# Loading each edge tile's query rows from DRAM in a two-layer graph transformer on one Trainium2 core

## What is computed

```
# layer 0                                    # layer 1 (edges carry 64 features)
h = layer_norm(x); q, k, v = h@Wq, h@Wk, h@Wv    q, k, v = x@Wq, x@Wk, x@Wv; e = edge_attr@We
logit = sum(q[dst] * k[src], -1) / 4             logit = sum(q[dst] * (k[src] + e), -1) / 4
p = exp(logit - segment_max(logit, dst)[dst])    the same
alpha = p / segment_sum(p, dst)[dst]             the same
agg = segment_sum(alpha * v[src], dst)           agg = segment_sum(alpha * (v[src] + e), dst)
x = x + agg@Wo + bo                              x = x + norm(x + agg + x@Wskip + ...) etc.
x = x + gelu(layer_norm(x)@W1 + bf1)@W2 + bf2    feed-forward with norms
```

## Time and profile before

| | |
|---|---|
| time, median of 3 runs | 1712.79 us (1712.45 to 1723.33) |
| profiled execution | 1715.09 us, of which 1713.4 us are the span from the first instruction to the last |
| TensorE busy, matrix products | 1117.7 us, 65% |
| VectorE / ScalarE / GpSimd busy | 1070.8 us, 62% / 842.6 us, 49% / 897.7 us, 52% |
| DMA | 222.70 MB, mean 130 GB/s |
| edge loop of the first layer | from about 60 to 762 us |
| edge loop of the second layer | from about 862 to 1610 us |

### The profile page before, as it was taken

One profiled execution on the slowest core, in us unless ns is written; L12 is line 12 of the kernel. 1 busy time (PEld: TensorE's weight loads), 2 busy tenths in 40 slices (PEclk: granted clock), 3 DMA queues, 4 the chain that ended last, 5 costly groups with the idle time before them and its releaser, 6 DMA issues. The chain is left out here.

```text
span 1713.4 us, 27206 instructions
## 1 busy us (share of the span) xinstructions
PE 1117.7 (65%) x6771; PEld 999.6 (58%) x6771; DVE 1070.8 (62%) x2749; ACT 842.6 (49%) x2617; POOL 897.7 (52%) x1001
## 2 busy tenths in 40 slices
PE   3504666656656666778941678777686777778675
PEld 2304566656656655667821667666575676767674
DVE  5505666666765666785710766667666676766866
ACT  1203554555565555574510255455545555555775
POOL 3572665666566666403467065655555555554044
PEclk9756876787778877788975878788878878777888
DMA  5642454445545544420133255545555554544101
GB/s 162 135 131 86 126 160 151 127 156 164 151 132 159 159 128 154 146 100 10 54 117 105 90 163 151 168 146 175 153 160 160 153 163 155 158 144 147 64 2 38
DMA packets 100397, 222.70 MB, mean 130 GB/s; under 512 B 34859, under 2 KB 49482, under 8 KB 96669
## 3 DMA queue, kind: packets, MB, share of 16 engines
...
## 5 line engine op out<-in xcount | busy, mean ns | idle before, releaser
L487 POOL DMA_INDIRECT KV<-kv_table,idx x832 | 803.6, 966 | 573.0 <-issue 459.3
L784 PE MATMUL PS<-QT,OHT 128*128 x1664 | 420.7, 342 | 291.0 <-issue 143.1
L784 PEld LDWEIGHTS PS<-QT,OHT 128*128 128x128 f32 x1664 | 331.8, 246 | 323.1 <-issue 321.6
L785 PE MATMUL PS<-QT,OHT 128*128 x1664 | 407.3, 334 | 16.2 <-issue 15.9
L785 PEld LDWEIGHTS PS<-QT,OHT 128*128 128x128 f32 x1664 | 334.0, 248 | 18.6 <-issue 18.6
L616 ACT ACTIVATE AGG<-AGG,PC,RCS x800 | 309.3, 387 | 2.5 <-ACT AGG L612 1.7
L1096 DVE TENSOR_TENSOR KV<-KV,PS 128x1024 f32<-128x1024 f32 x104 | 125.9, 1210 | 252.3 <-remote 204.2
L608 ACT ACTIVATE PC<-PS 128x4 f32<-128x4 f32 x200 | 34.2, 171 | 495.7 <-PE PS L830 243.5
L830 PE MATMUL PS<-OH,KV 128*128 128x128 f32 x1600 | 235.9, 296 | 45.1 <-issue 29.9
L830 PEld LDWEIGHTS PS<-OH,KV 128*128 128x128 f32 x1600 | 217.3, 211 | 52.8 <-issue 49.7
L1103 DVE TENSOR_TENSOR PR<-KV,PS 128x512 f32<-128x512 f32 x208 | 141.0, 678 | 157.0 <-issue 86.8
...
## 6 DMA issues: line engine op xcount, KB each, us to landing
...
```

The lines of the kernel that those rows point to most:

```text
L487: g.indirect_dma_start(KV[:, s, j, :], None, kv_table, bass.IndirectOffsetOnAxis(ap=idx[:, s, j:j + 1], axis=0)).then_inc(gathered[s][hh], 16)
L784: te.matmul(o, OHT[:, q // 2, 0, e0:e0 + P], QT[:, ds(blk, P)], start=True, stop=False)
L785: last = te.matmul(o, OHT[:, q // 2, 1, e0:e0 + P], QT[:, ds(blk + P, P)], start=False, stop=True)
```

## The change

The queries of a block no longer stay on the chip. `projected` and `next_queries` write them to one of four slots (`q_out`), and `store` sends them to a second DRAM table, `q_table`, of 3328 rows of 512 bytes. `rel` is now the distance from the destination of the tile's own first edge, 0 to 127. `load_queries(n)` on SyncE reads the first nodes of the 16 tiles into registers (two loads of eight) and issues 16 DMAs, each of the 128 rows of `q_table` from that node on, into one half of the double-buffered `QW`. With that the tile needs one one-hot matrix of 128 rows and one product. `OHT` has half the size, `one_hots1` one instruction where it had two, `one_hots` two where it had four. TensorE loads no registers, and waits for `q_loaded` before every eight tiles.

```diff
@@ -46,7 +46,7 @@
...
     rel_dram = nc.dram_tensor("rel_dram", (G, J * P), BF16, kind="Internal").ap()
-    block_dram = nc.dram_tensor("block_dram", (G, J), I32, kind="Internal").ap()
+    q_table = nc.dram_tensor("q_table", (NP + P, D), F32, kind="Internal").ap()
     window_dram = nc.dram_tensor("window_dram", (G, P, J * P), F32, kind="Internal").ap()
@@ -60,10 +60,10 @@
...
         Y = sb("Y", [P, NP])
-        QT = sb("QT", [P, NP + P])
+        QW = sb("QW", [P, 2, J, D])
         AGG = sb("AGG", [P, NP + P])
         KV = sb("KV", [P, SLOTS, J, 2 * D])
-        OHT = sb("OHT", [P, 2, 2, 8 * P])
+        OHT = sb("OHT", [P, 2, 8 * P])
         OH = sb("OH", [P, J * P])
@@ -143,7 +142,7 @@
...
         hT2 = [tail[:, 8 + k, D:2 * D] for k in range(2)]
-        hL = [tail[:, 10 + k, 0:D] for k in range(2)]
+        q_out = [tail[:, 10 + k, 0:D] for k in range(4)]
         last_windows = KV[:, (G - SLOTS) % SLOTS, 0:J // 2, :].rearrange("p j d -> p (j d)")
@@ -153,13 +152,12 @@
...
-        dst_edge = OHT[:, 1, 1, 0:T].bitcast(I32)
+        dst_edge = QW[:, 1, 0:4, :].rearrange("p j d -> p (j d)")[:, 0:T].bitcast(I32)
         prep = kv_flat[:, 2 * J * 2 * D:3 * J * 2 * D]
...
         relC = prep[0:TP, 1538:1794].bitcast(BF16)
-        blkC = prep[0:TP, 1794:1798].bitcast(I32)
         firstC, samerC, loopC, sameC = [prep[0:TP, 1798 + n * P:1798 + (n + 1) * P].bitcast(U8) for n in range(4)]
@@ -305,13 +304,13 @@
...
-            sp.wait_ge(*done("rel_made", 2))
+            sp.wait_ge(*done("consts_made", 16))
+            sp.dma_start(q_table[NP:NP + P, :], PM[:, :]).then_inc(S["pad_stored"], 16)
+            sp.wait_ge(*done("rel_made", 1))
             sp.dma_start(flat(rel_dram).rearrange("(p n) -> p n", p=TP), relC).then_inc(S["rel_stored"], 16)
-            sp.dma_start(flat(block_dram).rearrange("(p n) -> p n", p=TP), blkC).then_inc(S["rel_stored"], 16)
             sp.wait_ge(*done("gate_made", 3))
             sp.dma_start(gate_dram, gate_rows).then_inc(S["gate_stored"], 16)
-            sp.wait_ge(S["rel_stored"], 32)
-            sp.dma_start(block_row[:, :], row(flat(block_dram))).then_inc(S["block_loaded"], 16)
+            sp.wait_ge(S["rel_stored"], 16)
             sp.wait_ge(S["gate_stored"], 16)
@@ -320,9 +319,12 @@
...
                     sp.dma_start(kv_table[ds(n * P, P), :], kv_out[k]).then_inc(kv_stored[k], 16)
+                    sp.wait_ge(*done("q_made", n + (l * NB + 1)))
+                    sp.sem_inc(S["sp_go"], 1)
+                    sp.dma_start(q_table[ds(n * P, P), :], q_out[k]).then_inc(kv_stored[k], 16)
                 def stored(n, k):
-                    sp.wait_ge(kv_stored[k], n * 4 + (16 - 4 * k + 16 * kv_uses[k] * l))
+                    sp.wait_ge(kv_stored[k], n * 8 + (32 - 8 * k + 32 * kv_uses[k] * l))
                     sp.sem_inc(S["kv_free"], 1)
...
                 def indices(n):
@@ -333,10 +335,19 @@
...
                 def places(n):
-                    sp.wait_ge(*done("oht_ready", n * 2 + 2 * G * l))
-                    sp.wait_ge(*done("oht2_ready", n * 2 + 2 * G * l))
+                    sp.wait_ge(*done("oht_ready", n + G * l))
+                    sp.wait_ge(*done("oht2_ready", n + G * l))
                     sp.sem_inc(S["sp_go"], 1)
                     sp.dma_start(REL[:, :], rel_dram[ds(n, 1), :].broadcast_to([P, J * P])).then_inc(S["rel_loaded"], 16)
+
+                def load_queries(n):
+
+                    for hh in range(2):
+                        first = values(first_row, n * J + 8 * hh, 8, ENG.SP, N)
+                        sp.wait_ge(*done("qe_ready", 4 * n + (4 * G * l - 6 + 2 * hh)))
+                        sp.sem_inc(S["sp_go"], 1)
+                        for m in range(8):
+                            sp.dma_start(QW[:, n % 2, 8 * hh + m, :], q_table[ds(first[m], P), :]).then_inc(q_loaded[n % 2][hh], 16)
                 def row_gates(n):
@@ -379,7 +390,13 @@
...
                 pipelined(sp, (store, 2), (stored, 0), slots=4)
+                if l == 0:
+                    sp.wait_ge(S["pad_stored"], 16)
+                    sp.wait_ge(S["block_loaded"], 16)
+                    sp.wait_ge(*done("rel_made", 2))
+                load_queries(0)
                 places(1)
+                load_queries(1)
                 if l == 0:
@@ -408,6 +425,8 @@
...
                         store_windows(n - 1)
+                    if n + 2 < G:
+                        load_queries(n + 2)
@@ -436,7 +455,7 @@
...
             g.memset(SUG[:, :], 0.0).then_inc(S["consts_made"], 1)
-            g.memset(QT[:, NP:NP + P], 0.0).then_inc(S["consts_made"], 1)
+            g.memset(PM[:, :], 0.0).then_inc(S["consts_made"], 1)
             g.memset(minus_big[:, :], -BIG).then_inc(S["consts_made"], 1)
@@ -473,7 +492,7 @@
...
                 for k in range(4):
-                    pool.wait_ge(kv_stored[k], 16 * kv_uses[k] * (l + 1))
+                    pool.wait_ge(kv_stored[k], 32 * kv_uses[k] * (l + 1))
                 def gather(n):
@@ -588,11 +607,9 @@
...
                     act.wait_ge(*done("qe_ready", n * 4 + 4 * G * l))
-                    for nf in range(2):
-                        sc.activation(OHT[:, 1, nf, :], REL[:, 8 * P:16 * P], ACT.Abs, bias=minus_part[:, nf:nf + 1]).then_inc(S["oht2_step"], 1)
-                    for nf in range(2):
-                        act.wait_ge(*done("oht2_step", n * 2 + (2 * G * l + nf + 1)))
-                        sc.activation(OHT[:, 1, nf, :], OHT[:, 1, nf, :], ACT.Relu, bias=one_col[:, 0:1], scale=-1.0).then_inc(S["oht2_ready"], 1)
+                    sc.activation(OHT[:, 1, :], REL[:, 8 * P:16 * P], ACT.Abs, bias=minus_part[:, 0:1]).then_inc(S["oht2_step"], 1)
+                    act.wait_ge(*done("oht2_step", n + (G * l + 1)))
+                    sc.activation(OHT[:, 1, :], OHT[:, 1, :], ACT.Relu, bias=one_col[:, 0:1], scale=-1.0).then_inc(S["oht2_ready"], 1)
@@ -670,9 +687,9 @@
...
-                act.wait_ge(S["rel_stored"], 32)
-                act.wait_ge(*done("rel_made", 3))
-                act.wait_ge(S["block_loaded"], 32)
+                act.wait_ge(S["rel_stored"], 16)
+                act.wait_ge(*done("rel_made", 2))
+                act.wait_ge(S["block_loaded"], 16)
                 warm(ACT.Exp)
@@ -764,25 +781,20 @@
...
                         skip_part(b, w)
-                pe.wait_ge(S["block_loaded"], 32)
                 pe.wait_ge(*done("q_made", NB * (l + 1)))
...
-                blks = [None] * 8
-
                 def queries_of(n, q):
...
                     if q % 2 == 0:
-                        blks[:] = values(block_row, n * J + 4 * q, 8, ENG.PE, NP - P)
-                        pe.wait_ge(*done("oht2_ready" if q // 2 else "oht_ready", n * 2 + (2 * G * l + 2)))
+                        pe.wait_ge(*done("oht2_ready" if q // 2 else "oht_ready", n + (G * l + 1)))
+                        pe.wait_ge(q_loaded[n % 2][q // 2], 128 * (n // 2 + 1 + G // 2 * l))
                     pe.wait_ge(*done("prod_done", n * 4 + (4 * G * l + q - 1)))
                     for m in range(4):
-                        blk = blks[q % 2 * 4 + m]
                         o = PS[q % 2][:, m * P:(m + 1) * P]
                         e0 = ((4 * q + m) % 8) * P
-                        te.matmul(o, OHT[:, q // 2, 0, e0:e0 + P], QT[:, ds(blk, P)], start=True, stop=False)
-                        last = te.matmul(o, OHT[:, q // 2, 1, e0:e0 + P], QT[:, ds(blk + P, P)], start=False, stop=True)
+                        last = te.matmul(o, OHT[:, q // 2, e0:e0 + P], QW[:, n % 2, 4 * q + m, :], start=True, stop=True)
                     last.then_inc(S["qe_ready"], 1)
...
                 def edge_part(n, q):
@@ -992,13 +1004,11 @@
...
             before_edge, edge_dst, after_edge = [tiles(dstC[:, n:n + TK * P]) for n in range(3)]
-            v.tensor_scalar(blkC, edge_dst[:, :, 0], 7, 7, ALU.logical_shift_right, ALU.logical_shift_left).then_inc(S["rel_made"], 1)
             v.tensor_tensor(tiles(sameC), edge_dst, before_edge, ALU.is_equal).then_inc(S["loops_step"], 1)
...
             v.tensor_tensor(passC, edge_dst[:, :, P - 1], before_edge[:, :, 0], ALU.is_equal).then_inc(S["loops_step"], 1)
-            dve.wait_ge(*done("rel_made", 1))
-            v.tensor_tensor(tiles(relC), edge_dst, blkC.unsqueeze(2).broadcast_to([TP, TK, P]), ALU.subtract).then_inc(S["rel_made"], 1)
+            v.tensor_tensor(tiles(relC), edge_dst, edge_dst[:, :, 0:1].broadcast_to([TP, TK, P]), ALU.subtract).then_inc(S["rel_made"], 1)
             dve.wait_ge(*done("loops_step", 4))
@@ -1072,8 +1082,8 @@
                 def projected(n, k):
...
                     dve.wait_ge(*done("proj_ready", n + 1))
-                    v.scalar_tensor_tensor(QT[:, ds(n * P, P)], o[:, 0:D], 0.25, BB[:, 0:D], ALU.mult, ALU.add).then_inc(S["q_made"], 1)
                     dve.wait_ge(*done("kv_free", n - 3))
```

(8 more changed lines are left out.)

6 lines of the change are left out of this document (3 added, 3 removed).

## The result

The changed kernel took 1692.1 us (median of 4 runs, 1685.2 to 1698.0) where the kernel before took 1713.4 (median of 4): the ratio is 0.9855, with an interval of 0.9823 to 0.9887. That is 21 us less, where 53 were forecast. Its profiled execution took 1693.75 us, 1692.0 of them span.

What follows compares the result with a forecast made beforehand. The prediction took TensorE, held while GpSimd issues gathers, to set a half batch's pitch of 12.3 us. Its terms, -5 - 33 - 13 - 5 - 7 + 9 + 1 = -53 us, gave 1660 us, range 1612 to 1710.

Steps and rivals of the forecast that it cites:

- a hold: Both edge loops: while GpSimd issues gathers, TensorE's results come late, until 1.3 to 1.6 us after the last gather's issue.
- Store of the queries, +9: First stage: SyncE's extra store for each of 25 blocks makes VectorE wait 0.35 us a block, +9 us.
- First layer, steady, -5: First layer's 43 steady halves: GpSimd waits as before, only the excess over a 12.35 us pitch goes, -5 us.
- my third rival: With fewer records the hold misses the sums, GpSimd's first-layer waits shrink too; 1610 us, chance 0.07.
- Second layer, steady, -33: Second layer's 43 steady halves: shorter long waits remove three quarters of 45 us, -33 us (bounds 0 and -45).
- So 0: SyncE's 16 row loads a batch: issued early enough for the rows to land in time, so no cost.
- my fourth rival: SyncE's row loads hold TensorE as gathers do, some 4 us in 43 batches: +170 us, about 1830, chance 0.07.
- Start of the second layer's loop, -13: Fewer query records ahead of VectorE's first products, so the fourth comes at 946, not 956: -13 us (0 to -25).
- Start of the first layer's loop, -5: VectorE's fourth product moves from 137 towards 117, but the gather burst doesn't move: -5 us (0 to -12).
- Last rounds, -7, and the last store, +1: Both loops' rounds without gathers save -7 us (0 to -12); between the layers only the last query store shows, +1 us.
- The clock: TensorE's granted clock falls with half the queries gone, shrinking the second layer's 33 us gain to 5; about 1690, chance 0.12.
- The second rival: Gathers don't hold TensorE; the pitch is GpSimd's and something else ends the wait; 1710 us, within 1%, chance 0.14.

Runs made afterwards that it cites:

- c1: The changed kernel itself, run again beside the kernel before: 1703.9 us against 1731.1, ratio 0.9845.
- e9: The changed kernel with the second layer's first two edge parts of a batch moved behind the first half's sums on TensorE: 1696.7 us, ratio 0.9886.
- e2: The kernel before with one more 64 KB store behind each block's store, to a table nothing reads: 1377.0 us, ratio 1.0091.
- e7: The kernel before with the second query product of each tile left out (numbers differ): 1672.4 us against 1716.2, ratio 0.9751.
- e10: The changed kernel without the row loads of batches 2 to 25, products using old rows (numbers differ): 1683.4 us, ratio 0.9812.
- e8: The changed kernel with a 128 x 1 memset on GpSimd behind each gather, which left the gathers' spacing at 1.25 us: 1692.2 us, ratio 0.9868.
- e5: The changed kernel with GpSimd waiting for VectorE's query-key products before each eight gathers in each layer's first four batches: 1703.6 us, ratio 0.9829.
- e4: The changed kernel with SyncE's edge-gate stores and loads put ahead of places(1) and load_queries(1): 1372.1 us, ratio 1.0061.

## Why the prediction was wrong in size

- **What bounds the kernel: right where there is a hold.** In the changed kernel, in c1 and in e9 the first layer's pitch stays at 12.3 to 12.5 us although TensorE lost 74 us of work (in the changed kernel's profile). But I took the hold for a property of the kernel and of gathers. Gathers alone don't make it: three chips ran the same gathers at the same 1.25 us and held neither TensorE nor SyncE, and the kernel before takes 1364 us there.
- **Store of the queries, +9: right.** +10.0 in the result, first gather 10.5 us later in e2.
- **First layer, steady, -5: right in the result (-8.0), and partly by luck.** Products alone give 7.4 (e7). With the row loads left out it is +10 (e10), where sums that are early make GpSimd run two bursts together. I had argued that GpSimd "waits as before"; with less work on TensorE it sometimes doesn't. That can cost time: where the sums come early in e10 the layer gets slower, and not faster as in my third rival. In e7 early sums mostly cost nothing. When they cost is open.
- **Second layer, steady, -33: the step that failed is "So 0" for the row loads.** The relief itself was sized too low if anything: with everything that the change removes and no row loads the 43 halves take 39.6 us less (576.2 to 536.6, e10), close to my bound of 45; the products alone give 24.2 (e7), so by subtraction the halved one-hots and the register loads on TensorE are worth the other 15, where I had counted one one-hot of 0.75 us. The loads took 22.0 of the 39.6 back (558.6 against 536.6; 23.1 against e8 on the same chip). I had asked whether the rows land in time, and they do: in this loop the profile puts no wait of a product down to them. I hadn't asked what 16 more issues do to the others. With them the segment sums are made after TensorE is let go in 14 of 22 batches, without them in none of the 21 ahead of the last (7.3 us against 3.7 to alpha). This comes nearest to my fourth rival, to which I gave 0.07, at a quarter of its price and in one layer alone: 0.5 us a half, 1 us a batch, and not 4. I had also said there that the loads have as many packets as the gathers. They have three times as many, 144 a load against 48 a gather (110592 packets of SyncE's queue are missing from e10 with its 768 loads; the 832 gathers have 39936). That the loads cost the 22 us is shown by e10; how they do it is argued from these timelines, and whether their number or their packets count isn't shown. In the whole time little of it is seen: without the loads the kernel would gain 6 to 9 us, not 22, since the first layer gets slower. So the loads aren't the whole miss: the next item (11 us) and the last rounds (6 us) make half of it.
- **Start of the second layer's loop, -13: mis-sized, -2.3, the second step that failed.** The first product came at 40 us after the first gather (forecast 32, before 74). But I let the later records run at 1.3 us each: the 24 of the third quarter, taken up from 902.96 on, should have been there at 934 and were at 945.7, 1.8 us a record, after the end of the burst. So the fourth product came 3 us sooner and not 10. Why a record takes longer there than before isn't shown; 16 row loads that weren't there before run beside them. In e5, where GpSimd stands still in between, the same stretch is 13 us shorter.
- **Start of the first layer's loop, -5: -3.2,** with a wait that I had overlooked. The edge gates' stores stand behind load_queries(1) on SyncE, so GpSimd's gathers of batch 2 paused from 110 to 122 us. It cost nothing that can be seen, perhaps since a pause lets TensorE go; this was not shown, as e4 ran on a chip without the hold.
- **Last rounds, -7, and the last store, +1: mis-sized, -0.3 together** (+1.6 and -1.9). In e7, which has no store of queries, the stretch between the layers is 6.1 us shorter than in the changed kernel; how much of it is the stores I did not test.
- **The rivals.** The clock fell to 0.71 and 0.77, but it did not take the gain back: e10, at 0.78 in the second layer, has 40 us. It is part of why a long half stays long (queries and edge parts at the low clock, 5.7 us, in the timeline of 1130.36). The second rival, that the gathers hold nothing, fits the chips without the hold. Where there is one, e5 speaks against it: a pause in the gathers lets TensorE go, and the start is 13 us shorter. The rule on which this rival rested (the Trainium skill, "SBUF — State Buffer", section "SBUF: two separate sides") says that a compute operation can't slow a DMA, nor a DMA a compute operation. The chips without the hold agree. On the others TensorE is late beside gathers, but no run shows where it is held, so they don't refute the rule, and the prediction went too far in saying that they disagree.
